# Moving loads and zero fills across two stage changes of a four-stage decoder block on one core

## The chip, the cores and the metric

The kernel runs on one core of one Trainium2 chip. The metric is the device time of one execution in microseconds (us), with all four layers of the block in one launch.

## The reference

The input x has 16 batches of 128 tokens with 1024 channels, the context ctx the same shape. Four residual layers follow each other, and each branch is scaled by the tanh of one gate:

```
x = x + tanh(g_xattn[0]) * window_attention(layernorm(x), ctx)       # 8 heads, window 16, 128 channels = tokens
x = x + tanh(g_ffn[0])   * quantised_ffn(layernorm(x))               # int8 fake-quant, 1024 -> 1024 -> gelu -> 1024
x = x + tanh(g_xattn[1]) * lane_attention(layernorm(x), ctx)         # 1024-wide q, k, v, o; 32 heads x 4 lanes
x = x + tanh(g_ffn[1])   * swiglu_lora_ffn(layernorm(x))             # 2752 hidden, rank 16
```

The window attention treats the 128 tokens of a batch as channels and the 1024 features as time: q, k and v are 128x128 products over a 128x1024 tile, each position attends to 16 neighbours, and a 128x128 output product follows. The quantised layer normalises, rounds each row to 8 bits with its own scale, multiplies by rounded weights, applies gelu, and does that once more.

## The kernel before, in words

`gated_decoder` runs five stages one after the other, each in a block of its own. A block has one instruction stream per engine. It ends when every engine has finished its stream and whatever that stream waits for, and only then does the next block start.

**Stage 1, `projections` (lines 987 to 1389).** It needs only ctx and weights, so it comes first. It computes the keys and values of the third layer for all 2048 tokens (16 blocks of 128 output rows, each against 2048 columns in four chunks of 512), rounds the weights of the quantised layer, folds the query weights, and splits six small low-rank factors into a high and a low part ("stacks"). Every product is made of three: high x high, high x low, low x high.

- At the start SyncE loads the mixing rows and biases (four small transfers), then x tile 0, x tile 1 and the first weight block, then x tiles 2 to 15. There are two x slots. Tile n waits until tile n-2 is transposed (`xt`).
- ScalarE issues six loads of the factors first of all (line 1164).
- TensorE transposes x tiles with `turn`: tile n into one of two places of PSUM, ScalarE copies it out as the high part (`xh`, line 1169), VectorE subtracts for the low part (`xl`, line 1266), and tile n waits for tile n-2 to be through (`xtl`). From tile 12 on only one of the two places is free, and tile n waits for tile n-1.
- The biases go through 48 matmuls of one column (line 1380) before the first product. Then `products(0, 0)` begins. Four `turn`s are woven into each of its first three chunks.
- After the first product block ScalarE issues all 18 stores of the stacks (line 1204) and waits until they have landed, then goes on with weight block 2, its results and the first rounding (`rounded`). TensorE's second product block has a transpose of a rounded weight (`turn_weight`) ahead of its third chunk.
- At the end SyncE stores the last block of kv (1 MB) and waits until it has landed (line 1140).

**Stage 2, `window_attention` (lines 54 to 497).** SyncE issues x tile 0, four weights, four biases, one row of biases, the gate, then context tile 0, x 1, context 1, x 2 to 4. ScalarE fills `kbd` (128 x 8320) with zeros (line 249) and then waits for the weights and for all of GpSimd's masks (`c1`). GpSimd makes the masks, then raises the first variance to the power -0.5 (`power(0)`), and then fills the two `vbd` buffers (128 x 8320 each, line 242) with zeros, and only after both computes `power(1)`. VectorE's `norm(1)` waits for `power(1)`, and the selection of batch 0's scores stands behind it in VectorE's stream. Then a software pipeline over the 16 batches runs; the keys of each batch are spread into `kbd` by 8 transfers, the values into `vbd` by 8 more.

**Stage 3, `quantized_ffn_queries`.** SyncE loads x tile 0, the gate, a scale row, a bias row, x tile 1 and so on; VectorE takes the statistics of tile 0 (line 759) after `xl` and after GpSimd's identity (`c1` at 3). It reads what stage 2 stored.

**Stages 4 and 5**, `lane_attention` and `swiglu_ffn`, are not touched.

## Time and profile before

| | |
|---|---|
| median of 3 runs | 3290.72 us (3285.51 to 3298.68) |
| the profiled execution's own time | 3291.82 us |
| its span, first to last instruction | 3290.1 us |
| mean granted TensorE clock | 0.976 |
| TensorE matmul busy | 3107.4 us, 94% of the span |
| VectorE, ScalarE, GpSimd busy | 1852.3, 1053.5, 708.2 us |
| stage 1 ends, stage 2 starts | about 462.4 and 463.5 us |
| stage 2 ends, stage 3 starts | about 845 and 846 us |

Times in the profile are microseconds from the first instruction. PE is TensorE, PEld its weight load, DVE VectorE, ACT ScalarE, POOL GpSimd, SPq and ACTq the issuing of transfers from SyncE's and ScalarE's streams. A clock of 1.0 is 2.4 GHz, 0.5 is 1.2 GHz.

### The profile page before, as it was taken

To read this page: it belongs to the slowest core of one execution; us is meant where nothing else is said; L and a number is where in the kernel's file an instruction comes from. 1 tells how busy PE (TensorE), PEld (TensorE's weight loads), DVE (VectorE), ACT (ScalarE), POOL (GpSimd) and SP (SyncE) were. 2 spreads that over 40 slices of the span, in tenths; PEclk is the share of its full clock that TensorE was granted. 3 is DMA by queue.
4 is the path that set the end of the run, shared out by engine and by line. 5 is a ranking of instruction groups with operands and counts; after the bars stand their busy time and mean duration, and the time that the engine had idled before them with its cause. 6 is when DMAs were issued, how large, how long until landed. Compare 5 with 4: busy or idle time off the path is not lost. (4 is left out here: it accounts for less than half of the span.)

```text
span 3290.1 us, 51992 instructions
## 1 busy us (share of the span) xinstructions
PE 3107.4 (94%) x20493; PEld 2362.6 (72%) x20493; DVE 1852.3 (56%) x2538; ACT 1053.5 (32%) x1555; POOL 708.2 (22%) x587
## 2 busy tenths in 40 slices
PE   7999979989599998999999899999999999999999
PEld 6788855655267785666666678887788888777876
DVE  3111138878688838777777578787666665200000
ACT  2222233332233326554555333333433333200000
POOL 0000020000000004333333355554344442000000
PEclk9999989999799999999999999999999999999999
DMA  5334347676522222222223544444554446643342
GB/s 181 125 114 141 116 140 134 154 184 117 205 71 78 71 97 108 83 86 92 92 92 113 165 156 156 156 156 155 189 164 155 155 159 214 213 149 119 121 143 99
DMA packets 370423, 445.61 MB, mean 135 GB/s; under 512 B 157488, under 2 KB 264624, under 8 KB 367296
## 3 DMA queue, kind: packets, MB, share of 16 engines
q1 hardware_dynamic: 354048, 394.04, 38.1%
q10 hardware_dynamic: 16192, 49.04, 4.1%
q8 instruction: 126, 2.06, 0.3%
q14 instruction: 57, 0.47, 0.0%
HBM read 257.69 MB, written 176.79 MB: 132 GB/s over the span
## 5 line engine op out<-in xcount | busy, mean ns | idle before, releaser
L2762 PE MATMUL g_ps<-g_xs,g_wq 128*128 128x512 f32 x2616 | 627.3, 393 | 0.0
L2762 PEld LDWEIGHTS g_ps<-g_xs,g_wq 128*128 128x128 f32 x2616 | 487.0, 189 | 99.9
L2846 PE MATMUL g_ps<-g_wd,g_h 128*128 128x512 f32 x1536 | 355.5, 392 | 0.0
L2846 PEld LDWEIGHTS g_ps<-g_wd,g_h 128*128 128x128 f32 x1536 | 290.4, 189 | 62.9 <-issue 1.1
L2275 POOL TENSOR_TENSOR g_wq<-g_s,g_wq 128x512 fp32r<-128x512 f32 x168 | 242.8, 1455 | 200.7 <-ACT g_wq L2340 200.7
L2275 POOL TENSOR_TENSOR g_wq<-fe_wt,g_wq 128x512 fp32r<-128x512 f32 x125 | 180.0, 1440 | 238.0 <-ACT g_wq L2336 238.0
L2704 DVE TENSOR_TENSOR g_ta<-g_ps,g_ta 128x1024 f32<-128x1024 f32 x4 | 4.9, 1224 | 375.8 <-PE g_ps L2843 375.8
L1369 PE MATMUL kv_gps<-kv_xh,kv_wh 128*128 128x512 f32 x512 | 205.5, 401 | 1.0 <-DVE kv_xl L1266 1.0
L1369 PE MATMUL kv_gps<-kv_xh,kv_wl 128*128 128x512 f32 x512 | 200.7, 392 | 0.0
L1369 PE MATMUL kv_gps<-kv_xl,kv_wh 128*128 128x512 f32 x512 | 200.7, 392 | 0.0
L1665 ACT COPY a_pt<-a_tps 128x1024 f32<-128x1024 f32 x128 | 129.4, 1011 | 205.6 <-PE a_tps L1821 205.3
L946 PE MATMUL f_gps<-f_xt,f_qwh 128*128 128x256 f32 x1024 | 192.1, 288 | 1.4 <-DVE f_xt L841 1.4
L1821 PEld LDWEIGHTS a_tps<-h_ident,a_e 128*128 128x128 f32 x1024 | 110.4, 142 | 98.6 <-issue 83.4
L2340 ACT CAST g_wq<-g_s 128x512 fp32r<-128x512 f32 x168 | 100.4, 620 | 228.7 <-DVE g_s L2530 142.4
L946 PEld LDWEIGHTS f_gps<-f_xt,f_qwh 128*128 128x128 f32 x1024 | 160.1, 192 | 3.7 <-DVE f_xt L841 1.6
L1769 DVE TENSOR_TENSOR a_e<-a_ring,a_mx 128x1024 f32<-128x1024 f32 x128 | 156.7, 1224 | 7.6
L1684 ACT ACTIVATE a_e<-a_e 128x1024 f32<-128x1024 f32 x128 | 135.6, 1059 | 73.9 <-DVE a_e L1769 73.9
L1765 DVE TENSOR_REDUCE a_mx<-a_ring 128x8 f32<-128x1024 f32 x128 | 155.6, 1215 | 0.0
L946 PE MATMUL f_gps<-f_xt,f_qwl 128*128 128x256 f32 x512 | 144.8, 283 | 0.0
L1821 PE MATMUL a_tps<-h_ident,a_e 128*128 128x128 f32 x1024 | 140.5, 280 | 1.8 <-ACT a_pt L1665 1.8
L2336 ACT CAST g_wq<-fe_wt 128x512 fp32r<-128x512 f32 x125 | 77.2, 617 | 198.6 <-DVE fe_wt L2511 139.6
L2762 PE MATMUL g_ps<-h_b,g_wq 128*128 128x512 f32 x528 | 129.5, 393 | 0.8 <-DVE h_b L2496 0.8
(312 smaller groups left out, 5580.8 us busy)
## 6 DMA issues: line engine op xcount, KB each, us to landing
g_h<-g_hidden SPq DMA_DIRECT2D x176, 256.0 KB, 2.7
g_hidden<-g_h ACTq DMA_DIRECT2D x84, 512.0 KB, 3.6
fe_wt<-g_merged SPq DMA_DIRECT2D x43, 512.0 KB, 4.6
g_merged<-fe_wt SPq DMA_DIRECT2D x40, 512.0 KB, 3.6
kv<-kv_y SPq DMA_DIRECT2D x16, 1024.0 KB, 6.0
early_x<-x SPq DMA_DIRECT2D x32, 512.0 KB, 6.1
g_down<-fe_rows SPq DMA_DIRECT2D x22, 512.0 KB, 6.3
fe_wt<-g_down SPq DMA_DIRECT2D x22, 512.0 KB, 4.4
```

Of the source, the lines that this page charges most:

```text
L946: m = pe.matmul(gps[:, n % 2, 0:2 * P], l[:, n, k, :], xt[c % 2][:, p, k, :], start=(k == 0 and j == 0), stop=(k == NK - 1 and j == 2))
L1369: m = pe.matmul(gps[:, c, :], l[i][:, k, :], r[:, k, 512 * c:512 * c + 512], start=(k == 0 and a == 0), stop=(k == NK - 1 and a == 2))
L1665: act.copy(pt[:, c % 2, :, :], tps[:, :, :]).then_inc(S["te"], 1)
L1684: act.activation(e[:, c % 4, :, :], e[:, c % 4, :, :], ACT.Exp, scale=SCALE).then_inc(S["ex"], 1)
L1765: dve.tensor_reduce(mx[:, c % 2, :], ring[:, sl, :, :], AX.X, ALU.max).then_inc(S["mx"], 1)
L1769: dve.tensor_tensor(e[:, c % 4, :, :], ring[:, sl, :, :], mx[:, c % 2, :].unsqueeze(2).to_broadcast([P, U, P]), ALU.subtract).then_inc(S[" ...
L1821: m = pe.transpose(tps[:, u, :], e[:, c % 4, u, :], ident[:, :])
L2275: pool.tensor_tensor(wq[q % NQ][:, 1, :], src, wq[q % NQ][:, 0, :], ALU.subtract).then_inc(S["wl"], 1)
L2336: act.copy(place_free(q), raw_of(u, m)[:, 512 * a:512 * a + 512]).then_inc(S["wh"], 1)
L2340: act.copy(place_free(quarters(u) + k), sums[i][:, :]).then_inc(S["wh"], 1)
L2762: w = pe.matmul(ps[:, bank(u, to), :], wq[q % NQ][:, l, P * k:P * k + P], xs[j][:, r, k, :], start=(first and k == 0 and a == 0), stop=(la ...
L2846: w = pe.matmul(to, tile[:, p % RING, l, cols], wd[f][:, r, os], start=(f == 0 and a == 0), stop=False)
```

## The change

1. Stage 1, start: x tile 0 is loaded ahead of everything; the factors' loads are issued by ScalarE after it has handled x tiles 0 to 3 and the first weights. There are four x slots (two of them in the unused second result buffer), and the biases have a semaphore of their own (`braw`).
2. Stage 1, first product block: the biases go through 8 matmuls of three columns inside the first chunk. Tile 2 is transposed without a wait, tiles 12 and 14 go to the weights' PSUM place, and the weights of block 1 are made at the fourth chunk instead of the third. PSUM places move accordingly.
3. Stage 1: the 18 stores of the stacks are split. ScalarE issues nine, SyncE nine. ScalarE no longer waits there for their landing, but before its first `query_high`.
4. Stage 1, end: thirteen transfers of stage 2 (x tile 0, four weights, four biases, bias row, gate, context tiles 0 and 1) are issued by SyncE once the last weights are made, into addresses that stage 1 no longer uses and stage 2 keeps reserved. SyncE no longer waits for the stores of kv. That wait is in the middle of stage 2.
5. Stage 2, start: ScalarE zeroes half of `kbd`, VectorE the other half after `norm(0)`. ScalarE waits for one step of GpSimd's masks instead of five, TensorE for all of them only at batch 0's transposes. `power(0)` is ahead of the masks. The zeros of `vbd` are written in 2 x 13 pieces of 640 columns; `power(1)` still follows them all.
6. Stage 2, end: in the last two but one rounds, SyncE loads x1 tiles 0 and 1 for stage 3 into the context's slots, which are where stage 3 has its first two x tiles. Stage 3 does not load them.

```diff
 def window_attention(...)
-        names = ("consts c1 c2 ...
+        S = {n: s.sem(n) for n in names} | {"consts": WE["consts"]}
-                    sp.wait_ge(S["zv"], n + 1)
+                    sp.wait_ge(S["zv"], NJ // 5 * (n + 1))
-            load_x(0)
-            for i, w in enumerate((wq, wk, wv, wo)):
-                sp.dma_start(w4[:, i, :], w).then_inc(S["consts"], 16)
...
-            load_cond(0)
             load_x(1)
-            load_cond(1)
...
-            sp.wait_ge(S["zk"], 1)
+            sp.wait_ge(S["zk"], 2)
...
+                if b in (B - 3, B - 2):
+                    past(sp, "pk", 2 * b + 4)
+                    past(sp, "pv", 2 * b + 4)
+                    sp.dma_start(first["next"][b - B + 3][:, :], x_out[b - B + 3]).then_inc(WE["next"], 16)
                 if b == B // 2:
+                    sp.wait_ge(WE["kvout"], 16 * 2 * NK)
                     early_loads(sp)
...
             pool.wait_ge(S["c1"], 1)
+            def power(n): ...
+            power(0)
...
-            power(0)
             pool.wait_ge(S["xn"], 1)
             for i in range(2):
-                pool.memset(vbd[i][:, :, :], 0.0).then_inc(S["zv"], 1)
+                for j in range(0, NJ, 5):
+                    pool.memset(vbd[i][:, j:j + 5, :], 0.0).then_inc(S["zv"], 1)
             for n in range(1, B):
                 power(n)
...
-            act.copy(kbd[:, :, :], zero[:, 0:1]...).then_inc(S["zk"], 1)
-            act.wait_ge(S["c1"], 5)
+            act.copy(kbd[:, 0:H // 2, :], zero[:, 0:1]...).then_inc(S["zk"], 1)
...
             norm(0)
+            dve.memset(kbd[:, H // 2:H, :], 0.0).then_inc(S["zk"], 1)
...
 def projections(...)
             def load_x(n):
-                if n >= 2:
-                    sp.wait_ge(S["xt"], n - 1)
-                sp.dma_start(x[:, n % 2, :], x_in[n]).then_inc(xld[n % 2], 16)
+                if n >= 4:
+                    sp.wait_ge(S["xt"], n - 3)
+                sp.dma_start(xin[n % 4], x_in[n]).then_inc(xld[n % 4], 16)
...
             sp.wait_ge(S["low"], 1)
+            store_stacks(sp, jobs[3:], starts[3:], widths[3:])
             every_block(sp, step)
...
             load_rounded(NK - 1, 1, w3)
+            sp.wait_ge(S["wp"], NB)
+            sp.wait_ge(S["g"], NC * (NB - 1))
+            sp.wait_ge(S["wl"], NB)
+            window_loads(sp)
             store_query(NK - 1)
...
-            sp.wait_ge(S["out"], 16 * NB)
...
-            act.wait_ge(S["stacks"], 16 * 3 * len(jobs))
+            store_stacks(act, jobs[:3], starts[:3], widths[:3])
...
             def turn(n):
-                if n >= 2:
-                    pe.wait_ge(S["xtl"], n - 1 if n < 13 else n)
+                if n > 2:
+                    pe.wait_ge(S["xtl"], n - 1)
+                if n == 12:
+                    pe.wait_ge(S["bm"], 1)
...
 def quantized_ffn_queries(...)
+        def tile(n):
+            return early_x[n][:, :] if n < 2 else x[:, n % 4, :]
-            load_x(0)
...
-            load_x(1)
```

## Rows read from the trace of the kernel before

**Rows 1.** The page, busy time, share of the span and instructions

```profile
PE 3107.4 (94%) x20493; PEld 2362.6 (72%) x20493; DVE 1852.3 (56%) x2538; ACT 1053.5 (32%) x1555; POOL 708.2 (22%) x587
```

**Rows 2.** Windows: stretch, length, engines' busy time (x instructions), TensorE clock, DMA share, GB/s

```profile
0.00:50.00 50.00, 36.37 (x208) 31.54 (x208) 18.78 (x24) 15.69 (x17) 2.13 (x11) 0.93 0.54 177
```

**Rows 3.** Timeline of stage 1's start: start, us, engine, line, operation, [idle before <- releaser]

```profile
2.68 0.91 SPq L1076 DMA_DIRECT2D kv_x<-in_ctx_dram  x2
8.54 1.94 PE L1323 MATMUL kv_gps<-kv_ident,kv_x 128*128 128x128 f32 x8 [8.54 <-DMA kv_x<-in_ctx_dram]
10.51 21.28 SPq L1076 DMA_DIRECT2D kv_x<-in_ctx_dram  x6
...
14.16 1.97 PE L1323 MATMUL kv_gps<-kv_ident,kv_x 128*128 128x128 f32 x8 [1.97 <-DMA kv_x<-in_ctx_dram]
...
19.30 5.72 PE L1380 MATMUL kv_gps<-kv_braw,kv_mix 128*128 128x1 f32 x48
...
25.45 1.94 PE L1323 MATMUL kv_gps<-kv_ident,kv_x 128*128 128x128 f32 x8 [0.43 <-issue]
```

**Rows 4.** Timeline of the first product block: x tiles and its end

```profile
35.78 1.09 PE L1323 MATMUL kv_tps<-kv_ident,kv_x 128*128 128x128 f32 x8 [0.70 <-DMA kv_x<-in_ctx_dram]
...
41.41 1.22 DVE L1266 TENSOR_TENSOR kv_xl<-kv_gps,kv_xh 128x1024 fp32r<-128x1024 f32 x1 [2.23 <-ACT kv_xh L1169]
...
59.32 1.07 PE L1323 MATMUL kv_tps<-kv_ident,kv_x 128*128 128x128 f32 x8 [1.06 <-DVE kv_xl L1266]
...
62.84 1.06 PE L1323 MATMUL kv_tps<-kv_ident,kv_x 128*128 128x128 f32 x8 [1.06 <-DVE kv_xl L1266]
...
71.84 1.95 PE L1330 MATMUL kv_wps<-kv_mix,kv_wraw 128*128 128x128 f32 x16
```

**Rows 5.** Timeline after the stores of the stacks

```profile
85.55 1.01 ACT L1175 CAST kv_wh<-kv_wps 128x1024 fp32r<-128x1024 f32 x1 [12.76 <-DMA down_b_stack<-kv_parts]
91.59 1.03 PE L1339 MATMUL kv_tps<-kv_identb,kv_wq 128*128 128x128 bf16 x8 [6.91 <-DVE kv_wq L1294]
```

**Rows 6.** Windows, TensorE alone: after the wait for the biases, and after the stacks

```profile
25.40:31.00 5.60, 5.55 (x20) 0.50 0.29 94
91.50:96.00 4.50, 4.41 (x17) 0.51 0.15 58
```

**Rows 7.** SyncE's waits around the first stage change: us in total, times, longest

```profile
SPq L1004 <- DMA kv<-kv_y: 4.5, 1, 4.5
```

**Rows 8.** Timeline of stage 2's start

```profile
463.50 0.20 POOL L205 MEMSET w_zero<- 128x128 f32 x1 [460.45 <-POOLq L1004]
463.68 0.96 POOL L207 MEMSET w_kp<- 128x1040 f32 x1
463.74 7.12 ACT L249 COPY w_kbd<-w_zero 128x8320 f32<-128x8320 f32 x1 [6.46 <-POOL w_zero L205]
467.06 1.21 POOL L214 TENSOR_SCALAR_AFFINE_SELECT w_m_h<-w_hm 128x128 f32<-128x128 f32 x4
470.60 14.04 POOL L242 MEMSET w_vbd<- 128x8320 f32 x2 [0.91 <-DVE w_xn L308]
472.08 5.58 DVE L319 TENSOR_SCALAR w_m_p<-w_m_p 128x32 f32<-128x32 f32 x1
480.56 5.05 SPq L155 DMA_DIRECT2D w_kbd<-w_kp  x8
484.60 0.55 POOL L236 TENSOR_TENSOR w_rstd<-w_mv,w_half 128x1 f32<-128x1 f32 x1
488.67 0.64 DVE L336 COPY_PREDICATED w_sc<-w_pick,w_sps 128x128 f32<-128x128 int32 x2 [0.71 <-ACT w_sc L268]
501.77 1.72 PE L414 MATMUL w_prj<-w_cond,w_w 128*128 128x512 f32 x2 [1.95 <-DMA w_cond<-in_ctx_dram]
```

**Rows 9.** Timeline of stage 3's start

```profile
846.80 0.29 POOL L653 CAST f_identb<-f_ident 128x128 bf16<-128x128 f32 x1
849.42 1.29 DVE L759 BATCH_NORM_STATS2 f_st<-early_x 128x6 f32<-128x512 f32 x2 [7.66 <-DMA early_x<-x]
```

More of the change, by code:

```diff
@@ L68, in window_attention @@
         s = Scope(nc, ctx, "w")
-        x = s.sb("x", [P, XS, D])
-        cond = s.sb("cond", [P, 2, D])
+        reserved = s.sb("reserved", [P, 4 * D])
+        cond, w4, bias, bvr, g = (first[n] for n in ("cond", "w4", "bias", "bvr", "g"))
+        x = [first["x"], *(s.sb(f"x{i}", [P, D]) for i in range(1, XS))]
         xn = s.sb("xn", [P, D])
@@ L593, in load_x @@
                 sp.wait_ge(S["xl"], 16 * n)
[L594 removed]
+                sp.dma_start(tile(n), x_in[n]).then_inc(S["xl"], 16)
             def store(b):
@@ L1060, in every_block, with store_stacks @@
             step(NB - 2, 0, NB - 3, NK - 2, w3)
+        def store_stacks(eng, jobs, starts, widths):
+            for (a, o, which), at, width in zip(jobs, starts, widths):
+                R = a.shape[0]
+                for i, part in enumerate(which):
+                    eng.dma_start(flat(o[R * i:R * i + R, :]), parts[:, part, at:at + width].bitcast(F32)).then_inc(S["stacks"], 16)
         def ready(eng, *waits):
@@ L1188, in _ @@
             weights(0, 0)
-            act.wait_ge(S["bp"], 1)
-            act.copy(bmix[:, :], bps).then_inc(S["bm"], 1)
-            act.wait_ge(S["bm"], 1)
+            for (a, _, _), at, width in zip(jobs, starts, widths):
+                act.dma_start(factors[:, at:at + width], flat(a)).then_inc(S["factors"], 16)
             for c in range(NC):
@@ L1221, in query_high @@
                     act.wait_ge(S["qst"], 16 * j)
+                else:
+                    act.wait_ge(S["stacks"], 16 * 3 * len(jobs))
                 act.copy(qs[:, 0, :], wps[:, :, :].rearrange("p k n -> p (k n)")).then_inc(S["qwh"], 1)
@@ L1348, in query_weights, with biases @@
                 w.then_inc(S["qwp"], 1)
+            def biases():
+                pe.wait_ge(S["braw"], 32)
+                for k in range(NK):
+                    m = pe.matmul(bps.rearrange("p (a k) -> p k a", k=NK)[:, k, :], mix[:, k, :, :].rearrange("p g m -> p (g m)"),
+                                  braw[:, :].rearrange("p (a k) -> p k a", k=NK)[:, k, :], start=True, stop=True)
+                m.then_inc(S["bp"], 1)
             def products(n, i, between={}):
@@ L1367, in products @@
                             turn(4 * c + 4 + k // 2)
+                        if first and c == 0 and k == 4:
+                            biases()
                         for a, (l, r) in enumerate(((wh, xh), (wh, xl), (wl, xh))):
@@ L1378, in _ @@
             turn(3)
-            for n in range(NB + NK):
-                m = pe.matmul(bps[:, n:n + 1], mix[:, n % NK, :, :].rearrange("p g m -> p (g m)"), braw[:, n:n + 1],
-                              start=True, stop=True)
-            m.then_inc(S["bp"], 1)
             products(0, 0)
```

149 lines of the change are left out of this document (83 added, 66 removed).

## The prediction

> **What bounds the kernel now.** I read the page first. TensorE's matmuls are busy 3107.4 of 3290.1 us [rows 1], so a change can only pay where TensorE stands still. The windows by stage show where that is. In the first 50 us it is busy only 36.37, against 94% over the span [rows 1, 2]. Then I read the timeline at the places the diff touches: the start, the first product block, the stores of the stacks, and the two stage changes [rows 3 to 5, 8, 9]. Stages end in a barrier, so what is saved ahead of one is saved in full, unless TensorE's clock or a later wait takes it back.
>
> **Stage 1, start.** Tile 0 is issued third to last of six on SyncE, at 2.68, behind small loads and beside six factor loads, and TensorE starts at 8.54, 5.9 us later. Tile 2, issued alone at 10.51, is there at 14.16, 3.65 us later [rows 3]. Tile 0 now goes at 0.8, where the first small load went (2.68 less four issues of 0.47), with nothing beside it: TensorE starts at about 4.5. Tile 2 no longer waits for a slot and arrives behind 1.5 MB of others, at 8.4 by my estimate (tile 0 plus three tiles of 1.3 us). Then: transpose 2 to 10.3, weights to 12.9, transpose 3 to 13.9, ScalarE's and VectorE's last copies of 1.0 and 1.2 us each twice to 17.6. The 48 one-column matmuls (5.72) that held TensorE until 25.45 are gone from here. The first product block starts 25.45 - 17.6 = 7.8 us earlier. Bounds: 4 if the packed loads land one after another as late as tile 0 did, 9 if TensorE's clock is up already.
>
> **Stage 1, first product block.** It lasts from 25.45 to 71.84, 46.4 us [rows 3, 4]. A tile goes around TensorE 0.8, ScalarE 1.01, VectorE 1.22 with gaps: 62.84 - 59.32 = 3.52 us. Four tiles (12 to 15) share one PSUM place and each takes these 3.52; with two places each costs TensorE only its own transpose and six matmuls, 0.82 + 6 x 0.228 = 2.2. That is 4 x 1.3 = 5.3 us. Waits for x tiles, as the 0.70 at 35.78, of which there are three, go with four slots: 1.7. Added: 8 bias matmuls at 5.72/48 = 0.12, 1.0 us. What stays is one wait of about 1 us at each chunk's start, for VectorE's last subtraction, and the slow clock of the first 5 us [rows 6]. Sum 6.0 (4 to 7). TensorE's new wait for `bm` at tile 12 comes some 20 us after ScalarE's copy: nothing.
>
> **Stage 1, stacks.** ScalarE stood still 12.76 us until 18 stores were issued and landed, then came weights, scale and rounding, and TensorE waited 6.91 us at its third chunk [rows 5]; after that it ran 4.5 us at clock 0.51 [rows 6], 2.2 us lost. From ScalarE's restart at 85.55 to TensorE's at 91.59 are 6.0 us. Now ScalarE issues nine: 4.4 to 6.4 us (12.76/18 = 0.71 each at most), and does not wait. TensorE needs 12.7 us from 71.84 to its third chunk, ScalarE's path takes 5 to 7 + 6.0. SyncE's nine issues delay the first load to be rounded by the same 4.4 to 6.4 us, and it lands behind 2.2 MB of stores; that may be last. I leave a stall of 0.8, at full clock: gain 6.9 + 2.2 - 0.8 = 8.3, taken as 8.0 (bounds 4 and 9.1).
>
> **First stage change.** SyncE waits 4.5 us for kv to land [rows 7]. That goes; the thirteen early issues (6.2 us) lie in the last product block, where SyncE had only the last query store behind them. Their 2 MB compete with nothing TensorE needs. 4.5 us, bounds 4 and 5. The wait for `kvout`, put into round 8, is 150 us late: nothing. TensorE lost nothing else at this barrier.
>
> **Stage 2, start.** Times from its first instruction, 463.50 [rows 8]. Loads are no longer a term; TensorE makes keys at once. ScalarE's half fill lasts 3.6 (half of 7.12), key 0 is copied at 4.6, keys 1 at 7.5. VectorE has normalised at 3.6. Its fill of 4160 columns is in no row: 2.2 us at two elements per cycle (1024 in 0.81) and 4.4 at one (1024 in 1.22). I take 4.4, so `kbd` is zero at 8.0. Keys are spread from 8.0 instead of 17.06: 9 us. But GpSimd comes last. Its masks ended at 467.06 + 1.21, 4.8 after the start; `power(0)`, now ahead of them, waits for the statistics and adds 1.0: 5.8. The fills: 128 x 1040 in 0.96 against 7.02 for 8320 is 0.83 ns a column and 0.04 per instruction in a row, so 640 columns take 0.57, and 26 pieces 14.8 us: to 20.6. `power(1)` is queued behind them all, then 0.55; `norm(1)` 0.8; batch 0's selection starts at about 22.1 instead of 25.17: 3.1 us, not 9. Of this TensorE can lose some, as it stands still from 15 to 22 and restarts slow. Later the third context tile, which is loaded by then, saves up to 1.95 at 501.77. I take 3.8 in all; bounds -1.3 (below) and 5.5.
>
> The row of 5.58 us for a 128x32 VectorE operation that ends with GpSimd's first long fill (470.60 + 7.02) is a block by that fill [rows 8]. By the Trainium skill, SBUF — State Buffer, "Who interferes with whom", GpSimd and a VectorE operation that runs two elements a cycle hold one pair of ports exclusively, each for its whole instruction. The trace agrees, 5.58 us. Pieces of 0.57 end that, though nothing waited for the blocked operation, so it is no term.
>
> The same page says that a VectorE operation with no such mode does not meet GpSimd, and the Trainium skill, VectorE: DVE Perf Modes, "Zero memsets can be issued as uint32 (trn2)", gives one cycle per element for a fill. An estimate from the two: 4160/0.96 GHz = 4.33 us and no delay of the masks; the sum stays. No run here shows it yet.
>
> **Second stage change.** The store of the last tile is still waited for. VectorE's first statistics went at 849.42, waiting for x1; now the identity is last, 846.80 + 0.29 + 0.06 = 847.15 [rows 9]. 2.3 us (1.5 to 2.5); scale rows and second weights are issued 0.5 to 1 us earlier too, and were not waited for.
>
> **Sum.** 7.8 + 6.0 + 8.0 + 4.5 + 3.8 + 2.3 = 32.4 us. From the profiled execution's 3291.82 us (span 3290.1) that gives 3259.4. It lies 1.1 above the median, so I say 3259.5.
>
> **Rivals.**
> A. VectorE's fill blocks GpSimd's masks. They end 4.4 later, fills at 25.0, selection at 26.5 against 25.17: -1.3 in place of 3.8, 3264.5. For it: the 5.58 row shows that the two engines can block. Against it: reductions at one element a cycle ran beside the fill from 470.60 on.
> B. Transfers bound stage 1's start. With six 512 KB tiles packed, start gains 4, and SyncE's delayed load leaves 4 of the 8 at the stacks: 3259.5 + 3.8 + 4 = 3267. For it: tile 0's 5.9 us. Against: 2 MB packed move at some 400 GB/s, 1.3 us a tile.
> C. The clock pays it back, on the other side. Stages 4 and 5 are dense; if TensorE's mean clock fell from 0.976 to 0.96, 3107.4 us of matmul would grow by 1.7%, 52 us: 3311, slower. It decides from a fall of 0.01 (32 us). Against: low clocks in this trace follow idle stretches only [rows 6], and the change removes some.
> D. The change does less than it says: a wait I took for off the path (SyncE's in stage 2's start, where spreads of keys, values and the context load share one queue) holds both starts, and only the kv wait, the second change and the first product block pay: 12.8 us, 3279.
>
> **How the numbers follow.** Forecast 0.63, A 0.12, B 0.14, C 0.03, D 0.08. The forecast's own terms at their bounds give 3251 to 3268; A and B lie within it, so the range is 3250 to 3270. A measurement of this kernel tells 0.5% (16.5 us) from no change: faster than 3274.3 holds for forecast, A and B, and some of D: 0.91. Same 0.06, slower 0.03.
>
> **What would show it.** Right: the first products near 17.6; the second product block's third chunk without a long wait; stage 2 starting 4.5 us after less time; `power(1)` at about 21 us into stage 2 and VectorE waiting for it; VectorE's fill at 4.4 us; statistics in stage 3 about 1.1 us after its start. Wrong: a wait for x tiles in the first chunk, for a rounded weight's load after the stacks, or clock rows below 1.0 in dense stretches.

## The result, and the profile after

| | before | after |
|---|---|---|
| median | 3296.43 us of 6 runs (3285.51 to 3298.68) | 3272.12 us of 6 runs (3268.2 to 3277.08) |
| profiled execution, its span | 3291.82, 3290.1 us | 3268.2, 3266.5 us |
| mean granted TensorE clock | 0.976 | 0.979 |

The ratio is 0.9937, with a 95% interval of 0.9925 to 0.995. The change makes the kernel 0.6% faster, more than the 0.5% that can be told from nothing. But it saves 23.6 us of span where 32.4 were forecast, and 3272.12 lies 2 us above the range that was given. The two profiled executions, which the table of parts below compares, are each some 4 us faster than the median of their kernel (3291.82 against 3296.43, 3268.2 against 3272.12).

The page's busy line, and the first 50 us (PE, PEld, DVE, ACT, POOL, then clock, DMA share, GB/s), answer to [rows 1, 2]:

```profile
PE 3099.8 (95%) x20461; PEld 2356.9 (72%) x20461; DVE 1862.2 (57%) x2539; ACT 1050.2 (32%) x1555; POOL 708.4 (22%) x611
```

```profile
0.00:50.00 50.00, 36.98 (x217) 31.82 (x218) 21.50 (x26) 18.72 (x20) 2.12 (x11) 0.97 0.64 215
```

TensorE's busy time in the first 50 us hardly grew (36.37 to 36.98). The gain is in what it does there, as the timeline of stage 1's start shows (against [rows 3]):

```profile
4.63 1.94 PE L1348 MATMUL kv_gps<-kv_ident,kv_x 128*128 128x128 f32 x8 [4.63 <-DMA kv_x<-in_ctx_dram]
...
7.13 0.15 DVE L1275 TENSOR_SCALAR kv_am<-kv_am 128x1 f32<-128x1 f32 x1 [7.13 <-DMA kv_am<-in_L_xattn_amp_dram]
...
8.93 1.97 PE L1348 MATMUL kv_tps<-kv_ident,kv_x 128*128 128x128 f32 x8 [2.35 <-DMA kv_x<-in_ctx_dram]
9.34 1.23 DVE L1283 TENSOR_TENSOR kv_mix<-kv_mix,kv_ident 128x1024 f32<-128x1024 f32 x1
...
11.46 1.97 PE L1348 MATMUL kv_gps<-kv_ident,kv_y 128*128 128x128 f32 x8 [0.57 <-DMA kv_y<-in_ctx_dram]
...
13.22 2.04 PE L1355 MATMUL kv_wps<-kv_mix,kv_wraw 128*128 128x128 f32 x16
...
19.63 1.44 PE L1348 MATMUL kv_gps<-kv_ident,kv_x 128*128 128x128 f32 x8 [3.49 <-DVE kv_wl L1294]
```

Tile 0 is transposed at 4.63, 3.9 us earlier, as forecast (4.5). But tile 1 comes only at 8.93, and tile 2 at 11.46 (the line with `kv_y`, its slot), where 8.4 was forecast. From there on TensorE does not wait: tile 2, the weights at 13.22, tile 3 at 15.10, and 4.5 us later, when ScalarE and VectorE have copied tile 3 and the weights, the block starts. So tile 2's landing sets the start. The amplitude, one number spread over 128 rows, was issued behind tile 0 at 1.72 and is there only at 7.13, 5.4 us later, but the mixing matrix made from it is ready at 10.57, 2.6 us before the weights are multiplied by it: it is not on the path. What delays the tiles is seen in the transfers. From 4 to 6 us, while small loads and large ones are under way together, the DMA engines were busy 0.72 of the time and moved 91 GB/s; from 8 to 10 us they moved 411.

The first product block starts at 19.63 instead of 25.45: 5.8 us. In the eight profiles of the experiments that leave this start as it is, it starts at 20.17 to 21.27, 20.6 on average, so 5.8 is a lucky draw and 4.9 typical. The matmuls of the weights took 2.04 us here and 2.9 to 3.6 there.

The end of the first product block, and the place of the long wait after the stacks (against [rows 4, 5]):

```profile
61.09 1.95 PE L1355 MATMUL kv_wps<-kv_mix,kv_wraw 128*128 128x128 f32 x16
...
74.96 0.62 PE L1364 MATMUL kv_tps<-kv_identb,kv_wq 128*128 128x128 bf16 x8 [1.03 <-DVE kv_wq L1317]
```

The block takes 61.09 - 19.63 = 41.5 us (46.4 before). From its end to the transpose of the rounded weight are 13.87 us instead of 91.59 - 71.84 = 19.75. The wait is 1.03 instead of 6.91, and the eight transposes take 0.62 instead of 1.03: no half clock [rows 6]. What is left of the wait comes from the load of the weight to be rounded, which SyncE issues behind its nine stores: VectorE stands still 2.80 us for it, until 71.09.

The first stage change. SyncE's last store of kv is issued, and stage 2's first instruction follows 1.64 us later, where the wait for the landing was [rows 7]:

```profile
438.70 0.39 SPq L1114 DMA_DIRECT2D kv<-kv_y  x1
440.34 3.00 SPq L130 DMA_DIRECT2D w_x<-in_x_dram  x4
```

Stage 2's start, from 440.34 (against [rows 8], from 463.50):

```profile
443.22 0.85 POOL L213 TENSOR_SCALAR_AFFINE_SELECT w_hm<-w_hm 128x128 f32<-128x128 f32 x1
...
444.67 3.52 DVE L307 MEMSET w_kbd<- 128x4160 f32 x1 [0.81 <-issue]
...
446.52 14.96 POOL L236 MEMSET w_vbd<- 128x640 f32 x26
...
448.22 5.33 SPq L152 DMA_DIRECT2D w_kbd<-w_kp  x8
...
449.62 11.89 DVE L315 TENSOR_SCALAR w_m_p<-w_m_p 128x32 f32<-128x32 f32 x1
...
461.55 1.29 DVE L294 BATCH_NORM_STATS2 w_st<-w_x 128x6 f32<-128x512 f32 x2
...
463.42 0.55 POOL L208 TENSOR_TENSOR w_rstd<-w_mv,w_half 128x1 f32<-128x1 f32 x1 [1.94 <-DVE w_mv L298]
...
463.99 2.08 PE L410 MATMUL w_prj<-we_cond,we_w 128*128 128x512 f32 x2 [9.58 <-DVE w_vt L342]
...
467.87 0.64 DVE L332 COPY_PREDICATED w_sc<-w_pick,w_sps 128x128 f32<-128x128 int32 x2 [2.62 <-ACT w_sc L263]
```

The keys are spread 7.9 us after the start instead of 17.1. Then VectorE's small operation at line 315 lasts 11.89 us, until GpSimd's 26 fills are all over (446.52 + 14.96 = 461.48). It lasted 5.58 us before. Batch 1's statistics, its values and its second power stand behind it, GpSimd waits 1.94 us for the statistics, and TensorE 9.58 us for the values. The selection of batch 0 starts 27.5 us into the stage, later than the 25.17 of before.

The second change, where 7.66 us have become 4.84 [rows 9]:

```profile
825.21 1.29 DVE L766 BATCH_NORM_STATS2 f_st<-we_next 128x6 f32<-128x512 f32 x2 [4.84 <-POOL f_identb L660]
```

| part | forecast | profile |
|---|---|---|
| stage 1, start | 7.8 | 5.8 |
| first product block | 6.0 | 4.9 |
| stacks | 8.0 | 7.9 |
| first stage change | 4.5 | 4.5 |
| stage 2, start (to batch 1's transposes, 59.8 us in, 59.0 before) | 3.8 | -0.8 |
| steady part of stage 2 | 0 | -1.0 |
| second stage change | 2.3 | 2.8 |
| stage 3's first statistics to the end | 0 | -0.6 |
| sum | 32.4 | 23.5 |

The last part is scatter: it is almost all in stages that were not touched, and in the fourteen profiles of this case it lasts 2434.1 to 2444.5 us.

### The profile page after: what moved, and what is told of

Its sections match the earlier page's. It is cut to its first block and busy times, and to the rows that moved or that the text cites. A ratio compares the mean times of both kernels' runs of the same rounds, so it can differ in the third digit from the quotient of the medians.

```text
span 3266.5 us, 51970 instructions
## 1 busy us (share of the span) xinstructions
PE 3099.8 (95%) x20461; PEld 2356.9 (72%) x20461; DVE 1862.2 (57%) x2539; ACT 1050.2 (32%) x1555; POOL 708.4 (22%) x611
```

## Experiments: VectorE's blocked operation

My first theory was that pieces without a gap keep VectorE out, and that two whole fills let it in between them, as in the kernel before. A rival was that pieces or whole fills make no difference. All edits are made to the kernel after. Where no median is given, the kernel was executed once, and as single executions of one kernel lie up to 15 us apart, its time says little. The distances inside its profile are what is compared.

**Whole fills again.**

```diff
-                    sp.wait_ge(S["zv"], NJ // 5 * (n + 1))
+                    sp.wait_ge(S["zv"], n + 1)
...
-                for j in range(0, NJ, 5):
-                    pool.memset(vbd[i][:, j:j + 5, :], 0.0).then_inc(S["zv"], 1)
+                pool.memset(vbd[i][:, :, :], 0.0).then_inc(S["zv"], 1)
```

> The changed kernel with GpSimd's zeros of the two vbd buffers in two whole instructions again instead of 26 pieces. Theory (pieces issued without a gap keep the shared port from VectorE, so the 128x32 TENSOR_SCALAR waits for the last of them, 11.89 us): with two whole fills it gets in between them, so it lasts about 4 us (until the first fill ends, 13.2 us into stage 2), and batch 0's selection starts at about 22.5 us into the stage, when the power after the fills is through, instead of 27.5: 5 us earlier. Rival (the blocked operation is not on the path, the power behind the fills is): selection stays at 27 to 28. Rival (piece or whole makes no difference to who gets the port): it lasts about 11 us here too.

Measured: 3264.77 us, span 3262.6. Its timeline:

```profile
445.25 14.00 POOL L235 MEMSET w_vbd<- 128x8320 f32 x2
...
448.34 10.94 DVE L314 TENSOR_SCALAR w_m_p<-w_m_p 128x32 f32<-128x32 f32 x1
```

The operation ends with the second fill (459.25), not with the first, so the theory was wrong and the rival right. The block is about as long with two instructions as with 26: the pieces are not its cause, and they did not end it either, as I had said they would. The selection starts 26.6 us into the stage (465.63), 0.9 earlier, where the theory had 22.5.

**The operation on two inputs.** A row of ones is taken as the first input of a subtraction, so it is 1 - m as before.

```diff
+            pool.memset(one[:, :, :], 1.0)
...
-            dve.tensor_scalar(m_p[:, 1, :], m_p[:, 1, :], -1.0, 1.0, ALU.mult, ALU.add).then_inc(S["c2"], 1)
+            dve.tensor_tensor(m_p[:, 1, :], one[:, 0, :], m_p[:, 1, :], ALU.subtract).then_inc(S["c2"], 1)
```

> The changed kernel, pieces kept, with the one blocked 128x32 TENSOR_SCALAR of VectorE (one minus the sum of two masks) written as a subtraction of two tensors in SBUF, with a 128x32 tile of ones. Theory (the operation needs the port pair that the fills hold): it lasts 0.2 us, VectorE's statistics of batch 1 start about 9.5 us into stage 2 instead of 21.2, both value copies are done by 14 to 15, and selection of batch 0 starts at about 22.3 (behind the power that follows the fills) instead of 27.5. Rival (VectorE stood still there for another reason, such as the semaphore c2 or a slow memory): the new operation is as long.

Measured: 3272.76 us, span 3271.0, stage 2 from 442.87. The operation takes 0.19 us beside the same fills, and then:

```profile
452.21 0.19 DVE L317 TENSOR_TENSOR w_m_p<-w_one,w_m_p 128x32 f32<-128x32 f32 x1
452.44 1.28 DVE L296 BATCH_NORM_STATS2 w_st<-w_x 128x6 f32<-128x512 f32 x2
...
464.67 0.81 DVE L305 TENSOR_SCALAR w_xn<-w_x,w_mv,w_rstd 128x1024 f32<-128x1024 f32 x1 [8.22 <-POOL w_rstd L210]
```

Batch 1's statistics come 9.6 us into the stage instead of 21.2. What VectorE waits for now is the second power, behind all the fills, as the prediction had it. The selection starts at 465.39, 22.5 us in: the forecast said 22.1. The transposes of batch 1 come 55.8 us in, 4.0 us earlier than in the kernel after (five experiments that leave this code as it is have 59.6 to 61.1) and 3.1 earlier than in the one before (forecast 3.8). So the term of 3.8 was sized about right for a kernel without the block. The whole run shows no gain: its stage 1 happened to end 2.5 us later, the rest of its stage 2 took 330.1 us instead of 325.1, with more stretches at half clock at the end (below), and the later stages 0.9 more.

**The second power between the fills,** with the operation on two inputs, and `norm(1)` as one operation with the factor broadcast, so that the fills that still run can't block it:

```diff
                 for j in range(0, NJ, 5):
                     pool.memset(vbd[i][:, j:j + 5, :], 0.0).then_inc(S["zv"], 1)
-            for n in range(1, B):
+                if i == 0:
+                    power(1)
+            for n in range(2, B):
...
+                if n == 1:
+                    dve.scalar_tensor_tensor(out=xn[:, :], in0=x[n % XS][:, :], scalar=mv[:, 0:1],
+                                             in1=rstd[:, 0:1].to_broadcast([P, D]), op0=ALU.subtract, op1=ALU.mult).then_inc(S["xn"], 1)
```

> As e2, and in addition GpSimd computes the power of batch 1 after the first buffer's 13 pieces instead of after all 26, and VectorE normalises batch 1 with an operation of two tensor inputs (no wait for the port). Theory (the blocked operation and the power behind the fills are the two things that ate the early loads): selection of batch 0 starts at 16 to 17 us into stage 2 instead of 27.5, the third batch's keys 6 to 10 us earlier, and the execution is 6 to 11 us shorter than that of the changed kernel, about 0.990 of before. Rival (the chain of key spreads and value stores of batch 0 is as long as GpSimd's): selection gains, but batch 0's attend products start at most 3 us earlier.

Measured: 3256.12 us, median of 5 (3252.48 to 3264.82); ratio to the kernel before 0.989 (0.9866 to 0.9914). The profiled execution was the slowest of the five. Stage 2 starts at 441.87 in it:

```profile
455.59 0.55 POOL L210 TENSOR_TENSOR w_rstd<-w_mv,w_half 128x1 f32<-128x1 f32 x1
...
456.17 1.29 DVE L308 SCALAR_TENSOR_TENSOR w_xn<-w_x,w_mv,w_rstd 128x1024 f32<-128x1024 f32 x1 [0.84 <-POOL w_rstd L210]
...
458.61 0.64 DVE L340 COPY_PREDICATED w_sc<-w_pick,w_sps 128x128 f32<-128x128 int32 x2 [1.15 <-ACT w_sc L267]
```

The selection is 16.7 us into the stage, the transposes of batch 1 49.0 us, 10.8 earlier than in the kernel after. The interval of its ratio lies wholly below that of the change (0.9925 to 0.995). The kernel holds three edits, and how the gain beyond that of the operation on two inputs is shared between the other two was not measured.

**A gap between the fills.** GpSimd waits for each piece before it issues the next, and then, in a second kernel, for the first of two whole fills only. The VectorE operation is the old one in both.

```diff
                     pool.memset(vbd[i][:, j:j + 5, :], 0.0).then_inc(S["zv"], 1)
+                    pool.wait_ge(S["zv"], NJ // 5 * i + j // 5 + 1)
```

> The changed kernel, with GpSimd waiting for each of its 26 pieces to be complete before it issues the next. Theory (VectorE is shut out because the next fill is already queued when one ends, so any gap lets it in): the 128x32 TENSOR_SCALAR lasts under 1.2 us instead of 11.89, batch 1's statistics start about 10 us into stage 2 and batch 0's selection follows the power behind the fills, at 22.5 to 25 (each wait may lengthen the fills by 0.05 to 0.15 us a piece). Rival (the port is held through the whole series whatever the gaps): the operation still lasts 11 to 15 us and selection starts at 27 or later.

Measured: 3272.84 us, span 3271.1.

```profile
448.22 17.87 POOL L236 MEMSET w_vbd<- 128x640 f32 x26
...
451.31 0.33 DVE L316 TENSOR_SCALAR w_m_p<-w_m_p 128x32 f32<-128x32 f32 x1
```

The gaps cost GpSimd 2.9 us (17.87 against 14.96), and the block is gone: 0.33 us. But the second power waits for the longer fills. The selection starts 25.5 us in (22.5 to 25 expected), and the transposes of batch 1 come 59.0 us in, so this way out gains little.

```diff
-                    sp.wait_ge(S["zv"], NJ // 5 * (n + 1))
+                    sp.wait_ge(S["zv"], n + 1)
...
-                for j in range(0, NJ, 5):
-                    pool.memset(vbd[i][:, j:j + 5, :], 0.0).then_inc(S["zv"], 1)
+                pool.memset(vbd[i][:, :, :], 0.0).then_inc(S["zv"], 1)
+                pool.wait_ge(S["zv"], i + 1)
```

> Two whole fills as in e1, with GpSimd waiting for the first to be complete before it issues the second. In e1 the operation was blocked for 10.94 us, through both fills, and in the kernel before it got in after the first. Theory (a gap decides who is next): the operation ends with the first fill, 13.2 us into stage 2, so it lasts about 4.0 us, and batch 0's selection starts at about 22.5 instead of 26.6. Rival (who is next is decided by something older, as which engine asked first): again 10.9 us.

Measured: 3266.84 us, span 3265.1, with two whole fills and one wait between them:

```profile
448.38 3.97 DVE L315 TENSOR_SCALAR w_m_p<-w_m_p 128x32 f32<-128x32 f32 x1
...
459.49 0.55 POOL L208 TENSOR_TENSOR w_rstd<-w_mv,w_half 128x1 f32<-128x1 f32 x1
```

The operation ends at 452.35, with the first fill, and 7.0 us of block are gone against the whole fills without a wait. The selection starts 21.7 us in (22.5 expected), and the transposes of batch 1 come 54.4 us in (58.9 with the whole fills). The kernel after and these three (whole fills, a gap after each piece, one gap) agree: it is the lack of a gap between GpSimd's instructions that keeps VectorE out. One thing stays open, and no run settles it: in the kernel before, the two fills were back to back as well (14.04 us for both), and VectorE got in after the first [rows 8].

## Experiments: the start and the stacks

**Tile 1 first.** Is it the order of the loads that makes tile 1 late, and does it matter?

```diff
             load_x(0)
+            load_x(1)
             sp.dma_start(mt[:, :, :], mixing).then_inc(S["consts"], 16)
             sp.dma_start(am[:, 0:1], everywhere(amp, P)).then_inc(S["consts"], 16)
-            load_x(1)
```

> The changed kernel with x tile 1 issued directly behind x tile 0, ahead of the two small loads of mixing rows and amplitude. Theory (the small loads, in hundreds of packets under 512 bytes, hold up the large ones behind them): tile 1 is transposed at 6.6 to 7.3 us instead of 8.93, and the first product block starts about 1 us earlier than 19.63. Rival (the six tiles share one bandwidth whatever their order): tile 1 is there at 8 to 9 and the block starts within 0.5 us of 19.63; the amplitude then lands later than 7.1 and VectorE's mixing may hold the weights.

Measured: 3269.72 us, span 3268.0. From its timeline:

```profile
6.48 1.79 PE L1348 MATMUL kv_tps<-kv_ident,kv_x 128*128 128x128 f32 x8
...
7.82 0.15 DVE L1275 TENSOR_SCALAR kv_am<-kv_am 128x1 f32<-128x1 f32 x1 [7.82 <-DMA kv_am<-in_L_xattn_amp_dram]
...
10.62 1.26 PE L1348 MATMUL kv_gps<-kv_ident,kv_y 128*128 128x128 f32 x8 [2.36 <-DMA kv_y<-in_ctx_dram]
...
11.67 3.46 PE L1355 MATMUL kv_wps<-kv_mix,kv_wraw 128*128 128x128 f32 x16
```

Tile 1 is transposed 2.45 us earlier and tile 2 0.84 us earlier, and the weights are multiplied from 11.67 on, 1.55 us earlier, right behind tile 2's transposes. They take 3.46 us instead of 2.04, at a granted clock of 0.50 between 12 and 14 us, and the product block starts at 19.50 (19.63). Against the mean of 20.6 with the old order that is the 1 us that the theory had. The amplitude comes 0.7 us later and still does not bind: the mixing matrix is ready at 11.25. An execution with all stores on ScalarE (below) says the same from the other side. There the amplitude was ready at 5.65, 1.5 us earlier than in the kernel after, and the block started at 20.62.

**The small loads first.** The opposite order: mixing rows and amplitude ahead of tile 0, and the two biases behind tile 3.

```diff
+            sp.dma_start(mt[:, :, :], mixing).then_inc(S["consts"], 16)
+            sp.dma_start(am[:, 0:1], everywhere(amp, P)).then_inc(S["consts"], 16)
             load_x(0)
-            sp.dma_start(mt[:, :, :], mixing).then_inc(S["consts"], 16)
-            sp.dma_start(am[:, 0:1], everywhere(amp, P)).then_inc(S["consts"], 16)
             load_x(1)
             load_w(0, 0)
             load_x(2)
+            load_x(3)
             sp.dma_start(braw[:, 0:NB], bias).then_inc(S["braw"], 16)
             sp.dma_start(braw[:, NB:NB + NK], bq).then_inc(S["braw"], 16)
-            load_x(3)
```

> The changed kernel with the two small loads of mixing rows and amplitude ahead of x tile 0, and both bias loads behind x tile 3. Theory (behind large loads a small one takes 5.4 us, and hundreds of small packets hold up the tiles behind them): the amplitude is there at about 3.7 instead of 7.13, tile 1 is transposed by 8, tile 2 by 10.5 instead of 11.46, and the first product block starts at 18.3 to 19.0 instead of 19.63. Rival (the chain is bound by tile 0, which goes 0.9 us later): it starts at 19.6 or later.

Measured: 3269.52 us, span 3267.8.

```profile
4.15 0.15 DVE L1275 TENSOR_SCALAR kv_am<-kv_am 128x1 f32<-128x1 f32 x1 [4.15 <-DMA kv_am<-in_L_xattn_amp_dram]
...
9.68 1.24 PE L1348 MATMUL kv_gps<-kv_ident,kv_y 128*128 128x128 f32 x8 [0.16 <-DMA kv_y<-in_ctx_dram]
...
10.76 1.95 PE L1355 MATMUL kv_wps<-kv_mix,kv_wraw 128*128 128x128 f32 x16
...
17.07 1.97 PE L1348 MATMUL kv_gps<-kv_ident,kv_x 128*128 128x128 f32 x8 [3.49 <-DVE kv_wl L1294]
```

The amplitude is there 2.9 us after its issue instead of 5.4, and tile 0 1.2 us later. But tile 1 comes at 7.60 and tile 2 at 9.68, 1.3 and 1.8 us earlier: from 4 to 6 us the transfers run at 383 GB/s instead of 91. The weights follow tile 2 at once and take 1.95 us, and the block starts at 17.07, 2.6 us earlier (18.3 to 19.0 were expected). The forecast wanted 17.6. The two later kernels with this order start it at 18.63 and 17.14, so the mean gain is some 2.9 us against the mean of 20.6 with the old order. The edit moves the mixing rows and the amplitude ahead of the tiles and the biases behind them, and which of the two helps the tiles was not parted.

**All 18 stores by ScalarE,** without the wait. It parts the two halves of the old 12.76 us [rows 5]: issuing and landing.

```diff
-            store_stacks(sp, jobs[3:], starts[3:], widths[3:])
...
-            store_stacks(act, jobs[:3], starts[:3], widths[:3])
+            store_stacks(act, jobs, starts, widths)
```

> The changed kernel with all 18 stores of the low-rank factors issued by ScalarE again, none by SyncE, and still no wait there for their landing. Theory (issuing is the cost, landing is not): ScalarE is free about 12.5 us after the first product block's end instead of 4.9, and TensorE waits 5 to 7 us for the first rounded weight at the third chunk of the second block instead of 1.03, then runs some 4 us at half clock. Rival (the wait for landing was the cost): TensorE waits under 2 us.

Measured: 3274.42 us, span 3272.7.

```profile
72.99 2.34 ACTq L1082 DMA_DIRECT2D down_b_stack<-kv_parts  x3
75.44 1.01 ACT L1196 CAST kv_wh<-kv_wps 128x1024 fp32r<-128x1024 f32 x1 [12.73 <-PE kv_gps L1400]
...
81.48 1.04 PE L1363 MATMUL kv_tps<-kv_identb,kv_wq 128*128 128x128 bf16 x8 [6.87 <-DVE kv_wq L1316]
```

The issues run from 62.05 to 75.33, 0.74 us each, ScalarE stands still 12.73 us (12.76 before), and TensorE waits 6.87 (6.91). From the end of the first product block to the last store of kv it takes 7.4 us more than the kernel after, of the 7.9 that the change gained there. So the split of the issues over two queues is nearly all of it. What the wait for landing was worth by itself is not seen: in the kernel before the issues ended at 84.08 and ScalarE went on 1.5 us later, and here the issues took 1.3 us longer.

## Experiments: the stage changes, the clock and better versions

**Both start and second power.** The edits of the second power between the fills and of the small loads first, in one kernel.

> Three edits together: the second power of batch 1 between the two fills with the selection operation on two SBUF inputs and norm(1) as one operation with broadcast, and the two small loads ahead of x tile 0. Theory: they act in different stages and add up. The first product block starts near 17.1 (19.63 in the changed kernel), the transposes of batch 1 come about 49 us into stage 2 (59.8 in the changed kernel), so the profiled span is near 3260.5 or 2.5 us below that of the second power alone, ratio to the kernel before about 0.988. Rival: what the start gains is taken back at the wait for weights after the stacks or by a half-clock stretch, so the first stage ends no earlier than with the second power alone and the ratio stays at 0.989 to 0.990.

Measured: 3258.79 us, median of 4 (3253.49 to 3263.94); ratio 0.989 (0.9865 to 0.9915), no better than the second power alone. Its profile: tile 0 was late in this execution, and the product block started at 18.63.

```profile
6.57 1.94 PE L1356 MATMUL kv_gps<-kv_ident,kv_x 128*128 128x128 f32 x8 [6.57 <-DMA kv_x<-in_ctx_dram]
...
18.63 1.30 PE L1356 MATMUL kv_gps<-kv_ident,kv_x 128*128 128x128 f32 x8 [3.49 <-DVE kv_wl L1302]
```

Stage 2 starts at 438.98 (441.87 with the second power alone). Over all profiles with the stores split, stage 2 starts at 437.5 to 439.0 with the small loads in front (three kernels) and at 439.1 to 442.9 with the old order (the kernel after and six experiments). So the rival, which took the gain back within stage 1, is wrong; yet the forecast of the sum isn't shown either. Executions of one kernel differ by 10 us here, more than the 2.5 in question.

**Two waits back.** SyncE waits for kv's landing again, and x1's first two tiles are loaded after stage 2's last store.

```diff
             store(NB - 1, 1)
+            sp.wait_ge(S["out"], 16 * 2 * NK)
...
             sp.wait_ge(S["out"], 16 * B)
+            for i in range(2):
...
+                sp.dma_start(first["next"][i][:, :], x_out[i]).then_inc(WE["next"], 16)
```

> The changed kernel with two things undone: SyncE waits for kv to land at the end of stage 1 again, and x1 tiles 0 and 1 are loaded only when stage 2's last store has landed. Theory (each wait costs what it took at its barrier): the time from the last kv store's issue to stage 2's first instruction goes from 1.6 to about 6.1 us, the statistics of stage 3 start 1.5 to 2.8 us later than the 4.84 us after the last residual, and the profiled span grows by 6 to 7.3 us, to about 3273. Rival (part of it is hidden or made up later, as with stage 2's early loads): the distances at the two changes grow as said but the span grows by 3 us or less, because stage 2 starts with everything loaded or the clock is back earlier.

Measured: 3282.68 us, one run, span 3281.0.

```profile
440.32 0.39 SPq L1115 DMA_DIRECT2D kv<-kv_y  x1
446.48 1.76 SPq L130 DMA_DIRECT2D w_x<-in_x_dram  x4
```

```profile
838.21 1.29 DVE L767 BATCH_NORM_STATS2 f_st<-we_next 128x6 f32<-128x512 f32 x2 [8.45 <-POOL f_identb L661]
```

From the store to the stage are 6.16 us, 4.5 more, as said. The statistics of stage 3 come after 8.45 us, 3.6 more, above the 1.5 to 2.8, since this kernel also issues the two loads ahead of the barrier, one after the other, which the kernel before did not. The span grew by 14.5 us, where neither theory had more than 7.3: the two places give 8.1, and the other 6.4 are spread over the start (0.9), the rest of stage 1 (0.7), stage 2's start (1.3), its later part (1.9) and the later stages (1.5).

**Where such differences come from.** I read TensorE's clock in windows of 10 us through the steady part of stage 2, in every kernel. Two places are below 1.00. One is in all of them, in the middle of the stage; in the kernel after:

```profile
684.00:694.00 10.00, 6.56 (x40) 0.93 1.03 404
694.00:704.00 10.00, 4.97 (x16) 0.56 0.66 146
```

```profile
699.03 2.05 PE L410 MATMUL w_prj<-we_cond,we_w 128*128 128x512 f32 x2 [8.47 <-DMA we_cond<-in_ctx_dram]
```

(The columns are length, TensorE busy, clock, DMA share, GB/s.) TensorE stands still 8.47 us for a context tile, while the transfers run at 404 GB/s: round 8 issues 3 MB of stage 3's weights and rows ahead of that tile. With the wait and the slow clock the round takes 30.28 us, where the others take 21.03. The kernel before has the same wait, 8.10 us, and the round takes 29.52. The difference, 0.8 us, is most of the -1.0 of the table.

The other is the end of the stage, where the pipeline runs out and TensorE has short waits. Some executions drop to half clock once there, others two or four times. The same 36 us in the kernel after, and in the one with the small loads first, which is the same code there:

```profile
784.00:820.00 36.00, 25.04 (x480) 0.95 0.39 89
```

```profile
784.00:820.00 36.00, 26.77 (x470) 0.84 0.39 89
```

From batch 1's transposes to stage 3's statistics the first takes 325.11 us, the second 329.87. In windows of 2 us through the last 50 us of the stage, the eleven kernels with this code (the one after and ten of the experiments) fall into three groups. Three have one stretch at half clock and take 325 us, three have two and take 327 (the one with its two waits back less its 3.6), five have four and take 330. I found no relation to their edits. This is one part of what sets single executions apart. The later stages, which nothing touches, are another, with 2434 to 2444 us.

**The weights in pieces.** The wait in the middle, which nobody had touched:

```diff
-                if b == B // 2:
+                if b == B // 2 - 4:
                     sp.wait_ge(WE["kvout"], 16 * 2 * NK)
-                    early_loads(sp)
+                if there(b - B // 2 + 4) and b - B // 2 + 4 < NK + 2:
+                    early_loads(sp, b - B // 2 + 4)
...
-            sp.dma_start(ffn["wt0"][:, :, :, :], wt[0:NK].rearrange("o p k c -> p o k c")).then_inc(FE["wt0"], 16)
+                sp.dma_start(ffn["wt0"][:, n, :, :], wt[n]).then_inc(FE["wt0"], 16)
```

> The changed kernel, but the 2 MB of rounded weights and the two rows (1 MB) that stage 2 loads for stage 3 in its middle are issued one piece each round from round 4 to 13 (eight pieces of 256 KB, then the rows), behind the round's other transfers, instead of all in round 8 ahead of the context load. Theory: those 3 MB hold up the context load, which is why TensorE stands still 8.47 us at 699 and then runs at half clock until 703; with the pieces the wait goes, the clock stays at 1.00 there, and stage 2 is 9 to 10.5 us shorter: span near 3256.5, ratio to the kernel before 0.990 to 0.991. Rival: the queue is full anyway (DMA share 0.67 over the stage), so the added 256 KB a round make each round's context load or spread late by 0.5 to 1 us, ten times, and the span falls by 3 us or less.

Measured: 3261.78 us, median of 4 (3257.89 to 3270.23); ratio 0.9907 (0.9887 to 0.9927); span 3256.2 against the 3256.5 expected.

```profile
684.00:694.00 10.00, 10.00 (x89) 1.00 0.64 168
694.00:704.00 10.00, 9.00 (x216) 1.00 0.88 167
```

The wait and the slow clock are gone. Round 8 takes 21.03 us instead of 30.28, 9.25 less, and the other rounds still take 21.03, so the added 256 KB a round cost nothing. Batch 1's transposes to stage 3's statistics take 318.83 us instead of 325.11. That is 6.3 and not 9 to 10.5, as the clock at the stage's end was low for longer in this execution (0.74 and 0.84 in two windows of 10 us, and three stretches at half clock instead of one).

**All four edits together.**

> The second power between the fills, the selection operation on two inputs, the two small loads first, and the weights in pieces, all together. Theory: gains of different places add up, except that the short waits at the end of stage 2 may put the clock down two or three times (3 to 4 us in some executions). Span 3250 to 3255, ratio to the kernel before about 0.986. Rival: with batch 1 earlier the transfers of stage 2's first rounds bound it, or the context load of another round becomes late, and it is no faster than without the pieces (0.989).

Measured: 3247.04 us, median of 4 (3244.38 to 3251.95); ratio 0.9858 (0.9841 to 0.9875); span 3243.5, below the 3250 to 3255 expected. It beats both kernels: 1.4% under the kernel before, and its slowest execution is below the fastest of the kernel after (3268.2). No context load was late in its stage 2, and its end had one stretch at half clock, as in the kernel after: batch 1's transposes to stage 3's statistics take 315.97 us, 9.1 less than there, which is the gain of the pieces without the scatter. The kernel after was not timed beside this one, but each has a ratio to a kernel before that was, 0.9937 and 0.9858, and the two intervals lie apart.

## Why the prediction was wrong

Of the six parts three came out about as said in size and mechanism (the stacks and the two stage changes), two were too large, and one failed in its mechanism. The sum was 9 us too large. By its own steps:

- **Stage 2, start: the step that failed.** I read the 5.58 us row as a block by GpSimd's fill, and then wrote "Pieces of 0.57 end that, though nothing waited for the blocked operation, so it is no term". Both halves were wrong. The pieces ended nothing (11.89 us). And with loads, keys and values all early, VectorE's stream behind the blocked operation, batch 1's statistics and values, had become the path. It cost 4.0 us of the 4.6 that this term missed: with the operation unblocked, the selection starts at 22.5 (forecast 22.1). By the Trainium skill, SBUF — State Buffer, "Who interferes with whom", the engine that issues first has the pair for the whole instruction. For one instruction the trace of before agreed; the runs show that in a series without gaps the hold goes on, 10.94 us over two instructions and 11.89 over 26. I had counted the rule per instruction, where the row's end at one instruction's end invited it.
- **Stage 1, start: 7.8, measured 5.8.** "With nothing beside it" held for tile 0 (4.63, forecast 4.5). The step that failed is tile 2 "at 8.4 by my estimate (tile 0 plus three tiles of 1.3 us)": it came at 11.46, as the transfers moved 91 GB/s from 4 to 6 us and not the 400 of the estimate. Of these 3.1 us 1.1 came back behind it, 0.7 of them in the weights. With the small loads in front and the biases behind the tiles, tile 2 came at 9.68 and the block started at 17.1 to 18.6, about where I had wanted it (17.6).
- **First product block: 6.0, measured 4.9.** This is a size, and a slip in counting. The 48 in 5.72/48 are the profile's matmuls of one column, two for each of 24 in the kernel. The 8 matmuls of three columns that I added at that price are 16 in the profile, and took 1.85 us and not 1.0. The waits of 0.99 at the chunks' starts were foreseen. I ran no experiment on it.
- **Stacks: 8.0, measured 7.9.** Right, and by the reason given: the issues were the cost, which ScalarE's 18 issues without a wait show, and SyncE's load behind its nine stores came last ("that may be last").
- **First stage change: 4.5, measured 4.5,** and 4.5 more again when the wait is put back.
- **Second stage change: 2.3, measured 2.8.** The identity is last, as said, and loads ahead of the barrier are what moves it.
- **The rest, -1.6 of 0.** Of the -1.0 in stage 2, 0.8 is the context wait and its clock in round 8. This and the scatter at the stage's end were no term and no rival. Rival C named the clock, but for stages 4 and 5; where it did pay back in the experiments is stage 2's end, by 2 to 5 us. The -0.6 is within the scatter of the later stages.

Of the rivals, A came nearest in time (-1.3 at this place, where -0.8 was measured) by the wrong blocking. The masks ended 6.2 us into the stage against 4.8 before, of which the power ahead of them with its wait is 1.1. Beyond that, one mask operation took 0.85 us (0.35 before) beside `norm(0)`, VectorE's 128x1024 operation with one input. The three groups of masks beside VectorE's fill took as long as before (0.26, 0.46 and 1.21 us), so that fill held GpSimd up by nothing. The prediction had this from the Trainium skill, SBUF — State Buffer, "Who interferes with whom", where the sentence is for an operation with at most one input in SBUF; a fill has none. It was GpSimd's fills that held VectorE. B was half right: transfers did bound stage 1's start, by tile 2, and the start gained 5.8 (typically 4.9) against its 4 and my 7.8, but the 4 that it took from the stacks were not lost. D was not seen, the early starts did come.

The range was too narrow, and not by the terms' own bounds. Added up, these give gains of 16.2 to 38.1 us, so 3254 to 3276, and not the "3251 to 3268" that the prediction states; the measured 3272.12 and the profiled 3268.2 lie within them. And the forecast stood on an execution of 3291.82 us, near the median of the three runs known then, where the median of six is 3296.43. From that, the same gain of 32.4 us gives 3264, and the measured median lies 8 us above it instead of 12.6.

## What to carry to other kernels

When a stall is removed, look at every instruction in the stream behind it for the one that had been slow unnoticed: it may now be on the path, and its duration can change with what its neighbour does. Where an operation of VectorE is blocked by GpSimd's fills, give it two inputs or leave GpSimd a gap; shorter instructions alone did nothing. And count the smallest loads in the order of issue as carefully as the largest, as here four small ones among the tiles made the tiles behind them late (2.9 us of the start); but follow the waits back from the late instruction before naming the bound, for the amplitude, whose late landing stands out in the timeline, had 2.6 us to spare. A bulk load for a later stage goes in pieces behind the loads of each round, as 3 MB in one place cost 8.5 us of TensorE and its clock.

## What the hardware showed that I had not expected

- A VectorE operation over 128x32 with one input and constants waits for GpSimd's fills through a whole series: 11.89 us over 26 of them, 10.94 over two, 0.33 if GpSimd waits for each piece, 3.97 if for the first of two. The same subtraction with two inputs takes 0.19 us beside them. Of 128x1 operations with constants none was held up (0.15 us in all runs), nor was the 128x1024 operation with the factor broadcast (1.29 us). What two inputs do beside a GpSimd instruction that reads SBUF was not tried.
- The other way round, one GpSimd mask operation took 0.85 us instead of 0.35 in each of the thirteen profiles in which `norm(0)` ran beside it.
- VectorE's fill of 4160 columns took 3.52 us in every run, 0.85 ns a column, and GpSimd's masks beside it were not slowed. The Trainium skill, VectorE: DVE Perf Modes, "Zero memsets can be issued as uint32 (trn2)", has one cycle per element, for which the prediction's estimate was 4.33 us. The measured 3.52 is less, and it decides.
- One number spread over 128 rows landed 5.4 us after its issue behind a 512 KB tile (3.9 to 5.4 in nine profiles), and 2.9 us after it in front of one. With small loads among the tiles the DMA engines were busy 0.72 of the time from 4 to 6 us and moved 91 GB/s; with two of them in front and two behind, 0.96 and 383.
- Stores issued by ScalarE cost it 0.50 to 0.97 us each in the run with all 18 and no wait, 0.74 on average, and 0.44 to 1.25 in the kernel before.
- TensorE at its two levels: in the steady rounds the granted clock was 1.00, and it fell to 0.50 after 8.47 us of standing still, for about 4 us of work. At the stage's end, where TensorE's waits are 1 to 3 us, it fell once in some executions and four times in others, and single executions of one kernel lie up to 15 us apart (the one before: 3283.67 to 3298.85).
